# Joining the two half sums of a mixture-of-experts layer in PSUM, by identity products on TensorE, in place of an add on VectorE

## The chip, the cores and the metric

The kernel runs on one core of one Trainium2 chip. The metric is the device time in microseconds (us) of one execution, median of several runs. Its engines are TensorE (PE; its weight loads are PEld), VectorE (DVE), ScalarE (ACT), GpSimd (POOL) and SyncE (SP), which only issues DMAs here.

## The reference

Two post-norm transformer layers over 4 x 512 tokens of width 256, in float32. What matters here is the first feed-forward, a mixture of eight experts whose outputs are weighted by gates (two of the eight are not zero) and summed before one output projection:

```python
expert_out = gelu(einsum('bsh,ehd->ebsd', x, expert_w) + expert_b)
combined   = einsum('bse,ebsd->bsd', gates, expert_out)
y          = einsum('bsd,df->bsf', combined, out_w) + out_b
x          = layernorm(x + y)
```

## The kernel before

The 2048 tokens are 16 tiles of 128. The kernel is written out by hand for each engine, with semaphores; within an engine everything runs in the order in which it is written. All projections are three bf16 products (high x high, high x low, low x high, lines 468 to 470), which is why every activation is split into a bf16 high part (by ACT) and a low part (by DVE).

The first feed-forward is a software pipeline of steps, n = 0 to 17, from about 243 to 388 us of the span. Step n holds the experts of tile n, the first projection and norm of tile n + 6, and the end of tile n - 1 and n - 2. In PE's order a full step is:

1. the turn (transpose) "x1" of tile n + 5;
2. `experts(n, 0)` with the experts' bias (line 714), the first projection of tile n + 6, `experts(n, 1)`; every fourth step (n = 3, 7, 11) also router logits of four tiles, the "routed" steps below;
3. the turn "cc" of tile n + 7, then `experts(n, 2)`;
4. the turn **"cm"** of tile n - 1: the sum over the experts is turned so that it can be multiplied by `out_w`;
5. `experts(n, 3)`, the turn "x2" of tile n - 2, and `second_project(n - 1)`, which waits for DVE's low part of the turned sum.

First projections end with step 9, "cc" turns with step 8, "x1" turns with step 10. In step 16, where the experts are done, the first projections of layer 1 (`l1_project`: "k", "q", then "v" of one group) stand around the last "cm" turn, and step 17 has more of them.

The sum over the experts is made by two engines. DVE scales and adds the shares of experts 0 to 4 into `comb[t % 2]` (lines 1611 and 1614, semaphore `mul`), POOL those of experts 5 to 7 into `pc[t % 2]` (lines 2021 and 2026, semaphore `psum`). In step n DVE then joins the halves of tile n - 1, between `mix(n, 0)` and the residual add and statistics of `joined(n + 6, 1)`:

```python
dve.wait_ge(m["psum"], (NX - DVE_X - 1) * (t + 1))
dve.wait_ge(m["mul"], DVE_X * (t + 1))
dve.tensor_tensor(comb[t % 2], comb[t % 2], pc[t % 2], ALU.add).then_inc(m["join"], 1)
```

PE waits for `join` and turns the 256 columns in two fp32 transposes (line 667). ACT takes the high part from the bank (line 1062), DVE the low part (line 1381, `turned_low`, after the norms of the step). POOL may overwrite `pc` of tile t once tile t - 2 is joined.

DVE's order in a full step is: low part of x1, residual and statistics of tile n - 2 (lines 1507, 1509, 1510), `mix(n, 0)`, **join (line 1620)**, residual and statistics of tile n + 6, low part of cc, `mix(n, 1)`, the norms of tiles n - 2 and n + 6 (line 1516), low part of cm, `mix(n, 2)`, the next attention context (line 1493), low part of x2. In a routed step the choice of the experts (lines 1362 to 1376, 1546 to 1550) follows the low part of cm. POOL makes the inverse deviations for both norms (lines 2035, 2037).

Of the kernel before, what the change touches and what calls it, by code (L numbers as in the profile page):

```python
# [7 lines left out]
ALU = mybir.AluOpType  # L8
# [3 lines left out]
P = 128  # L12
E = 256
KE = E // P
# [3 lines left out]
NT = NB * TT  # L18
# [5 lines left out]
NX = 8  # L24
# [46 lines left out]
DVE_X = 5  # L71
# [18 lines left out]
TURNS = [(what, t) for at in sorted(EARLY_AT) for what, t in EARLY_AT[at] if what in ("cc", "x1")]  # L90
# [60 lines left out]
def build(nc, x_tok_d, x_t_d, wqkv_d, wall_d, const_d, bp_d, outb_d, b2_d, rb_d, eb_d, rw0_d, rw1_d, b1_d, out_d):  # L151
    ctx = ExitStack()
    with ctx:
# [3 lines left out]
        def sem(name):  # L157
            return ctx.enter_context(nc.semaphore(name))
# [46 lines left out]
        ident_f = consts[:, 0:P]  # L205
# [13 lines left out]
        lg = lg_sb[:, :].rearrange("p (t x) -> p t x", x=NX)  # L219
        rt = s_sb[0][:, 0:8 * NT * NX].rearrange("p (i c) -> p i c", i=8)  # L220
        gates = s_sb[0][:, 1152:1280].rearrange("p (t x) -> p t x", x=NX)
# [30 lines left out]
        def tiles(base, n, width, dt=F32):  # L252
            return [scr[:, base + width * i:base + width * (i + 1)].bitcast(dt) if dt != F32
                    else scr[:, base + width * i:base + width * (i + 1)] for i in range(n)]
# [5 lines left out]
        comb = tiles(1536, 2, E)  # L260
        tb_hi, tb_lo = tiles(12288, TB, P, BF16), tiles(13184, TB, P, BF16)
        ge = tiles(8192, 4, 512)
        pc = tiles(10240, 2, E)
# [27 lines left out]
        bank = [ctx.enter_context(nc.psum_tensor(f"bank{i}", [P, 512], F32)) for i in range(8)]  # L291
# [24 lines left out]
        def hold(eng, semaphore, value):  # L316

            if value > 0:
                eng.wait_ge(semaphore, value)
# [11 lines left out]
        l1_turned = [sem(f"l1_turned{i}") for i in range(2)]  # L331
        m = {n: sem(f"mix_{n}") for n in (
            "rc", "cc", "tp", "thi", "tlo", "o1", "o2", "r1", "r2", "agg1", "agg2", "rstd1", "rstd2", "x1", "x2", "xb",
            "lg", "lgc", "lgd", "ex", "gates", "f", "ge", "mul", "join", "pmul", "psum", "dve", "pool")}
        e = {n: sem(f"ffn_{n}") for n in (
            "tp", "thi", "tlo", "lg", "lgc", "lgd", "ex", "picks", "rank", "gates", "h", "ge", "hhi", "hlo",
            "y", "yr", "bg", "xb", "seq", "agg", "rstd", "x", "dve", "iota", "iotad", "rhi", "rlo", "pick",
# [4 lines left out]
        def turn_bank(i):  # L342
            return 7 if i < LONE_TURNS else i % 2
# [121 lines left out]
        def _(pe):  # L465
# [186 lines left out]
            def turn_mix(kind, t):  # L652

                i = TURNS.index((kind, t))
                if kind == "cc":
                    pe.wait_ge(m["cc"], t + 1)
                    src = cc[t % 2]
                elif kind == "cm":
                    pe.wait_ge(m["join"], t + 1)
                    src = comb[t % 2]  # L660
                else:
                    pe.wait_ge(m[kind], t + 1)
                    src = x_tok[:, t * E:(t + 1) * E]

                hold(pe, m["tlo"], i if i < LONE_TURNS else i - 1)
                for k in range(KE):
                    last = pe.transpose(bank[turn_bank(i)][:, k * P:(k + 1) * P], src[:, k * P:(k + 1) * P], ident_f)
                last.then_inc(m["tp"], 1)

            def project(out, t_hi, t_lo, base, n=E):  # L670
# [49 lines left out]
            for _ in range(WARM):  # L720
                pe.matmul(bank[7][:, :], ones_b[:, :], ones_b[:, :].unsqueeze(1).to_broadcast([P, TT, P]),
                          start=True, stop=True)
# [34 lines left out]
            for n in STEPS[len(EARLY):]:  # L757
                here, ahead, behind = 0 <= n < NT, n + LEAD + 1, n - 1
# [620 lines left out]
        def _(dve):  # L1379
# [4 lines left out]
            for i in range(2):  # L1384
                dve.memset(q_tok[i][:, :, M_ROW:ROWS], 0.0)
                last = dve.memset(k_tok[i][:, :, M_ROW + 3:ROWS], 0.0)
# [87 lines left out]
            def turned_low(kind, t):  # L1474
                i = TURNS.index((kind, t))
                dve.wait_ge(m["thi"], i + 1)
                if kind == "x2":
                    hi, lo = xt_hi[:, :, t * P:(t + 1) * P], xt_lo[:, :, t * P:(t + 1) * P]
                else:
                    his, los = {"cc": (ta_hi, ta_lo), "cm": (tc_hi, tc_lo), "x1": (tb_hi, tb_lo)}[kind]  # L1480
                    slot = t % (TB if kind == "x1" else 2)
                    hi, lo = kt(his[slot]), kt(los[slot])
                low(lo, kt(bank[turn_bank(i)][:, 0:E]), hi).then_inc(m["tlo"], 1)
# [35 lines left out]
            def sums_inverse(half):  # L1519

                heads = slice(half * NH // 2, (half + 1) * NH // 2)
                dve.wait_ge(a["vc"], (half + 1) * NT // 2)
                dve.reciprocal(rcc[:, heads, :], ctx0[:, heads, :, D0:VC].rearrange("p h q d -> p h (q d)")
                               ).then_inc(m["rc"], 1)
                dve.wait_ge(m["rc"], half + 1)
# [88 lines left out]
                        ins = dve.scalar_tensor_tensor(comb[t % 2], part, gate, comb[t % 2], ALU.mult, ALU.add)  # L1614
                    ins.then_inc(m["mul"], 1)

            def join_halves(t):
                dve.wait_ge(m["psum"], (NX - DVE_X - 1) * (t + 1))
                dve.wait_ge(m["mul"], DVE_X * (t + 1))
                dve.tensor_tensor(comb[t % 2], comb[t % 2], pc[t % 2], ALU.add).then_inc(m["join"], 1)  # L1620

            def l1_low(which, g, j=0):
                half = (g % 2) * TOK
                if which == "q":
                    hold(dve, c["phi"], 4 * g + j + 1)
                    low(qt_lo[j % 2], bank[4][:, :], qt_hi[j % 2]).then_inc(c["plo"], 1)
                elif which == "k":
                    hold(dve, c["kvh"], 2 * g + 1)
                    low(k1_lo[:, ds(half, TOK)], bank[5][:, :], k1_hi[:, ds(half, TOK)]
                        ).then_inc(c["kvl"], 1)  # L1630
                else:
                    hold(dve, c["kvh"], 2 * g + 2)
                    low(v1_lo[:, ds(half, TOK)], bank[5][:, :], v1_hi[:, ds(half, TOK)]
                        ).then_inc(c["kvl"], 1)

            for n in STEPS[len(EARLY):]:
                here, ahead, behind = 0 <= n < NT, n + LEAD + 1, n - 1
                if 0 <= n + LEAD < NT:
                    turned_low("x1", n + LEAD)
                if n == EARLY[-1] + 1:  # L1640
                    sums_inverse(1)
                if n == NT:
                    l1_low("k", 0)
                if 0 <= n - 2:
                    joined(n - 2, 2)
                routed = 0 <= n + 4 < NT and (n + 4) % TT == TT - 1
                if routed:
                    route((n + 4) // TT)
                if here:
                    mix(n, 0)  # L1650
                if 0 <= behind < NT:
                    join_halves(behind)
                if 0 <= ahead < NT:
                    joined(ahead, 1)
                if 0 <= n + LEAD + 2 < NT:
                    turned_low("cc", n + LEAD + 2)
                if n == NT:
                    l1_low("q", 0, 0)
                if here:
                    mix(n, 1)  # L1660
                if n == NT + 1:
                    l1_low("k", 1)
                if 0 <= n - 2:
                    norm(n - 2, 2)
                if n == NT + 1:
                    l1_low("v", 1)
                if 0 <= ahead < NT:
                    norm(ahead, 1)
                if 0 <= behind < NT:
                    turned_low("cm", behind)  # L1670
                if routed:
                    choose_first((n + 4) // TT)
                if n == NT:
                    l1_low("v", 0)
                if here:
                    mix(n, 2)
                if routed:
                    choose_second((n + 4) // TT)
                    gate((n + 4) // TT)
                if 0 <= n + LEAD + 3 < NT:  # L1680
                    context(n + LEAD + 3)
                if 0 <= n - 2:
                    turned_low("x2", n - 2)
# [179 lines left out]
            for i in range(2):  # L1863
                dve.wait_ge(e["yhi"], i + 1)
                cols = slice(2 * i * E, 2 * (i + 1) * E)
# [33 lines left out]
        def _(pool):  # L1899
            pool.memset(ones_b[:, :], 1.0).then_inc(c_ready, 1)  # L1900
            for i in range(2):
                last = pool.memset(k_tok[i][:, :, M_ROW:M_ROW + 3], -1.0)
# [108 lines left out]
            def mix(t, p):  # L2011

                pool.wait_ge(m["ge"], 4 * t + p + 1)
                if p == 2:

                    hold(pool, m["join"], t - 1)
                    if t % TT == 0:
                        pool.wait_ge(m["gates"], t // TT + 1)
                for x in range(max(2 * p, DVE_X), 2 * p + 2):
                    share = pc[t % 2] if x == DVE_X else pc_x[x % 2]  # L2020
                    pool.tensor_scalar(share, ge[p][:, (x % 2) * E:(x % 2 + 1) * E], gates[:, t, x:x + 1], 1.0,
                                       ALU.mult, ALU.mult).then_inc(m["pmul"], 1)
                    if x > DVE_X:
                        pool.wait_ge(m["pmul"], (NX - DVE_X) * t + x - DVE_X + 1)
                        hold(pool, m["psum"], (NX - DVE_X - 1) * t + x - DVE_X - 1)
                        pool.tensor_tensor(pc[t % 2], pc[t % 2], share, ALU.add).then_inc(m["psum"], 1)
# [146 lines left out]
```

## Time and profile before

| | |
|---|---|
| median of 3 runs | 892.85 us (892.05 to 892.85) |
| the profiled execution | 893.67 us, span 891.8 us |
| PE busy | 817.7 us, 92% of the span |
| DVE busy | 693.9 us, 78% |
| ACT, POOL busy | 496.5 us, 56%; 391.0 us, 44% |
| line 1620, the join, in the span | 16 instructions, 6.68 us |

Busy time of PE is a modelled sum: a matmul's end lies behind the start of the next one, so the distance between starts is the time that one takes when others follow. "Idle before" in square brackets is time of the engine ahead of an instruction, with what ended it.

### The profile page before, as it was taken

What the parts mean: (1) busy time and instruction counts of PE and PEld (TensorE: products, weight loads), DVE (VectorE), ACT (ScalarE), POOL (GpSimd) and SP (SyncE); (2) the same over time, 40 slices, a digit from 0 to 9 for tenths busy, and PEclk for the clock granted to TensorE, in tenths of its full rate; (3) what the DMA queues carried; (4) which work ended last, traced back from release to release, by engine and by line L of the source; (5) the groups of instructions that cost most, each with busy time, mean ns of one, the idle gap of its engine ahead of it and who ended that gap; (6) DMA issues with size and microseconds to landing.
All of it is one profiled execution on the core that took longest, in us unless ns stands there. A gap on an engine that the chain in (4) does not pass through costs nothing.

```text
span 891.8 us, 21987 instructions
## 1 busy us (share of the span) xinstructions
PE 817.7 (92%) x8131; PEld 514.1 (58%) x8227; DVE 693.9 (78%) x1921; ACT 496.5 (56%) x1181; POOL 391.0 (44%) x731
## 2 busy tenths in 40 slices
PE   7899999997898988979999999999999999997894
PEld 2455555553454544445566767666767766685374
DVE  4777777777688887678999888888888888856535
ACT  3577677765544534456666555656555565532243
POOL 4555667552365664523333343333333333333454
PEclk9999999999999999999999999999999999998998
DMA  5353333420000000016766565565556655550502
GB/s 167 107 127 91 94 84 97 121 31 8 2 1 1 1 1 1 1 28 122 119 123 123 97 104 104 99 101 98 96 99 103 104 105 97 97 91 1 95 1 95
DMA packets 219034, 67.70 MB, mean 76 GB/s; under 512 B 211360, under 2 KB 214704, under 8 KB 218928
## 3 DMA queue, kind: packets, MB, share of 16 engines
q1 hardware_dynamic: 218928, 66.29, 37.4%
q8 instruction: 66, 1.08, 0.5%
q14 instruction: 40, 0.33, 0.1%
HBM read 17.92 MB, written 4.19 MB: 25 GB/s over the span
## 4 chain that ended last, share of the span: by engine, by line
PE 71%; DVE 13%; issue 5%; DMA 3%; ACT 3%; POOL 3%; SPq 0%; POOLq 0%; DVEq 0%; ACTq 0%
PE bank L469 15%; PE bank L470 14%; PE bank L468 13%; PE bank L601 4%; PE bank L836 4%; PE bank L838 4%; PE bank L837 4%; DVE nm L1439 3%; DMA att<-w_lo 2%; PE bank L548 2%; PE bank L543 2%; PE bank L524 2%; PE bank L585 1%; DVE w_lo L1463 1%; DVE scr L1614 1%
## 5 line engine op out<-in xcount | busy, mean ns | idle before, releaser
L1157 ACT ACTIVATE att<-att,nm 128x512 f32<-128x512 f32 (+3 forms) x256 | 141.5, 553 | 104.4 <-DVE nm L1452 103.0
L1062 ACT ACTIVATE scr<-bank 128x512 bf16<-128x512 f32 (+3 forms) x210 | 111.5, 550 | 86.5 <-PE bank L838 44.2
L469 PE MATMUL bank<-w_lo,scr 128*128 128x256 bf16 (+1 forms) x478 | 144.0, 301 | 0.5
L468 PE MATMUL bank<-w_hi,scr 128*128 128x256 bf16 (+1 forms) x471 | 141.5, 300 | 2.9 <-DVE scr L1381 1.9
L470 PE MATMUL bank<-w_hi,scr 128*128 128x256 bf16 (+1 forms) x476 | 143.2, 301 | 0.1
L1439 DVE TENSOR_REDUCE nm<-bank 128x1 f32<-128x512 f32 (+3 forms) x256 | 110.6, 484 | 37.9 <-PE bank L548 37.8
L2070 POOL TENSOR_SCALAR wqkv_hi<-att,rr 128x512 bf16<-128x512 f32 (+3 forms) x128 | 66.1, 536 | 136.2 <-DVE rr L1469 136.2
L1452 DVE CUSTOM_DVE_ANT_0 att<-bank,consts 128x512 f32<-128x512 f32 (+3 forms) x256 | 113.2, 483 | 14.9 <-PE bank L470 14.9
L1108 ACT ACTIVATE att<-bank 128x512 f32<-128x512 f32 (+1 forms) x192 | 90.8, 528 | 50.1 <-PE bank L585 49.7
L1381 DVE TENSOR_TENSOR scr<-bank,scr 128x256 bf16<-128x256 f32 (+1 forms) x146 | 77.4, 540 | 51.0 <-ACT scr L1062 50.6
L2070 POOL TENSOR_SCALAR w_hi<-att,rr 128x512 bf16<-128x512 f32 (+3 forms) x128 | 66.1, 535 | 106.2 <-DVE rr L1469 106.2
L836 PE MATMUL bank<-att,w_hi 128*128 128x384 bf16 (+2 forms) x320 | 84.0, 273 | 4.5 <-DMA att<-w_lo 3.4
L837 PE MATMUL bank<-att,w_hi 128*128 128x384 bf16 (+2 forms) x320 | 87.2, 273 | 0.0
L838 PE MATMUL bank<-att,w_lo 128*128 128x384 bf16 (+2 forms) x320 | 83.9, 273 | 0.0
L469 PE MATMUL bank<-w_lo,w_hi 128*128 128x512 bf16 (+3 forms) x256 | 76.6, 299 | 0.5 <-DVE w_lo L1381 0.5
L470 PE MATMUL bank<-w_hi,w_lo 128*128 128x512 bf16 (+3 forms) x256 | 73.3, 299 | 0.0
L468 PE MATMUL bank<-w_hi 128*128 128x512 bf16 (+1 forms) x255 | 72.9, 299 | 0.2 <-DVE xt_lo L1381 0.2
L1381 DVE TENSOR_TENSOR w_lo<-bank,w_hi 128x512 bf16<-128x512 f32 x96 | 66.4, 691 | 8.2 <-ACT w_hi L1062 7.6
L1062 ACT ACTIVATE w_hi<-bank 128x512 bf16<-128x512 f32 x96 | 55.9, 582 | 28.1 <-PE bank L470 28.1
L469 PE MATMUL bank<-xt_lo,w_hi 128*128 128x512 bf16 x176 | 66.7, 379 | 3.1 <-DVE w_lo L1381 0.8
L1189 ACT ACTIVATE scr<-bank 128x512 f32<-128x512 f32 x64 | 38.1, 597 | 55.9 <-PE bank L470 35.0
L470 PE MATMUL bank<-xt_hi,w_lo 128*128 128x512 bf16 x176 | 66.7, 379 | 0.0
(242 smaller groups left out, 2014.7 us busy)
## 6 DMA issues: line engine op xcount, KB each, us to landing
scr<-wall_in SPq DMA_DIRECT2D x19, 512.0 KB, 4.7
v_by_token<-scr SPq DMA_DIRECT2D x16, 128.0 KB, 1.8
scr<-v_by_token SPq DMA_DIRECT2D x16, 128.0 KB, 3.5
x_tok<-x_tok_in SPq DMA_DIRECT2D x4, 512.0 KB, 5.1
scr<-x_t_in SPq DMA_DIRECT2D x3, 512.0 KB, 5.7
out<-x_tok SPq DMA_DIRECT2D x3, 512.0 KB, 2.6
scr<-wqkv_in SPq DMA_DIRECT2D x2, 384.0 KB, 3.6
att<-w_hi SPq DMA_TRANSPOSE x32, 3.4
```

Of the source, the lines that this page charges most:

```text
L468: pe.matmul(out, l_hi, r_hi, start=start, stop=False, skip_group_check=check)
L469: pe.matmul(out, l_hi, r_lo, start=False, stop=False, skip_group_check=check)
L470: return pe.matmul(out, l_lo, r_hi, start=False, stop=stop, skip_group_check=check)
L836: pe.matmul(out, v1_hi[:, vs], hi, start=(kt, q0) == (0, 0), stop=False, skip_group_check=True)
L837: pe.matmul(out, v1_hi[:, vs], lo, start=False, stop=False, skip_group_check=True)
L838: last = pe.matmul(out, v1_lo[:, vs], hi, start=False, stop=(kt == TT - 1), skip_group_check=True)
L1062: return act.activation(out, in_, ACT.Copy)
L1157: last = act.activation(at, at, ACT.Exp, bias=nm[:, j % 2, qt:qt + 1], scale=-1.0, accum_out=rs[:, j % 2, qt:qt + 1])
L1381: return dve.tensor_tensor(out, bank_cols, hi, ALU.subtract)
L1439: last = dve.tensor_reduce(nm0[:, p % 2, h, qt:qt + 1], bank[n % 2][:, col:col + w], AX.X, ALU.max)
L1452: last = dve.tensor_tensor_reduce(s_sb[j % 2][:, S_OFF[qt]:S_OFF[qt] + w], bank[turn][:, col:col + w], mask[:, 512 - w:512], -scale, HUGE, ...
L2070: pool.tensor_scalar(ps_hi[j % 2][:, at], s_sb[j % 2][:, at], rr[:, j % 2, qt:qt + 1], 1.0, ALU.mult, ALU.mult).then_inc(c["row"], 1)
```

## The change

The join leaves DVE. PE no longer transposes the joined sum: it multiplies each half by the fp32 identity, both into the same columns of the bank, so that PSUM adds them. There are four fp32 matmuls (two halves, two column blocks) in place of two transposes. The first pair waits for DVE's last share (`mul`), the second for POOL's last add (`psum`). POOL's guard on `pc` becomes the turn "cm" of tile t - 2.

```diff
                 elif kind == "cm":
-                    pe.wait_ge(m["join"], t + 1)
+                    pe.wait_ge(m["mul"], DVE_X * (t + 1))
                     src = comb[t % 2]
...
                 hold(pe, m["tlo"], i if i < LONE_TURNS else i - 1)
-                for k in range(KE):
-                    last = pe.transpose(bank[turn_bank(i)][:, k * P:(k + 1) * P], src[:, k * P:(k + 1) * P], ident_f)
+                if kind == "cm":
+                    halves = (comb[t % 2], pc[t % 2])
+                    for part, half in enumerate(halves):
+                        if part == 1:
+                            pe.wait_ge(m["psum"], (NX - DVE_X - 1) * (t + 1))
+                        for k in range(KE):
+                            cols = slice(k * P, (k + 1) * P)
+                            last = pe.matmul(bank[turn_bank(i)][:, cols], half[:, cols], ident_f,
+                                             start=(part == 0 and k == 0), stop=(part == 1 and k == KE - 1),
+                                             skip_group_check=True)
+                else:
+                    for k in range(KE):
+                        last = pe.transpose(bank[turn_bank(i)][:, k * P:(k + 1) * P], src[:, k * P:(k + 1) * P], ident_f)
                 last.then_inc(m["tp"], 1)
...
-            def join_halves(t):
-                dve.wait_ge(m["psum"], (NX - DVE_X - 1) * (t + 1))
-                dve.wait_ge(m["mul"], DVE_X * (t + 1))
-                dve.tensor_tensor(comb[t % 2], comb[t % 2], pc[t % 2], ALU.add).then_inc(m["join"], 1)
...
-                if 0 <= behind < NT:
-                    join_halves(behind)
...
                 if p == 2:
-                    hold(pool, m["join"], t - 1)
+                    if t >= 2:
+                        pool.wait_ge(m["tp"], TURNS.index(("cm", t - 2)) + 1)
```

On TensorE, at the turn "cm" of the tile before, between two pieces of experts (512 columns each) and ahead of the turn "x2"; before:

```order
L470 MATMUL bank<-w_hi,scr 128x512
L667 MATMUL bank<-consts,scr 128x128 [waits mix_tlo,mix_join]
L667 MATMUL bank<-consts,scr 128x128
L468 MATMUL bank<-w_hi,scr 128x512
L469 MATMUL bank<-w_lo,scr 128x512
```

and now:

```order
L470 MATMUL bank<-w_hi,scr 128x512
L673 MATMUL bank<-consts,scr 128x128 [waits mix_tlo,mix_mul]
L673 MATMUL bank<-consts,scr 128x128
L673 MATMUL bank<-consts,scr 128x128 [waits mix_psum]
L673 MATMUL bank<-consts,scr 128x128
L468 MATMUL bank<-w_hi,scr 128x512
```

Two instructions have become four, with the second wait in the middle; what stands around them is as before.

## Rows read from the trace of the kernel before

**Rows 1.** Page, part 1: busy time, share of the span, instructions.

```profile
PE 817.7 (92%) x8131; PEld 514.1 (58%) x8227; DVE 693.9 (78%) x1921; ACT 496.5 (56%) x1181; POOL 391.0 (44%) x731
```

**Rows 2.** Steps 6 to 12 and 15: stretch: length, busy us (instructions), granted clock, DMA.

```profile
core 0: us, PE busy (x) PEld busy (x) DVE busy (x) ACT busy (x) POOL busy (x), PEclk, DMA share, GB/s
294.22:302.34 8.12, 7.92 (x48) 4.46 (x49) 7.06 (x20) 3.60 (x9) 5.48 (x11) 1.00 0.00 0
302.34:312.45 10.11, 8.71 (x71) 4.93 (x73) 8.21 (x23) 6.89 (x13) 6.68 (x13) 1.00 0.01 2
312.45:322.93 10.48, 8.55 (x48) 4.22 (x49) 9.82 (x34) 3.73 (x9) 4.60 (x9) 1.00 0.00 2
322.93:330.64 7.71, 7.66 (x45) 4.20 (x46) 6.27 (x18) 2.71 (x7) 5.32 (x11) 1.00 0.01 2
330.64:337.58 6.94, 6.89 (x41) 3.69 (x41) 5.65 (x14) 3.20 (x8) 4.68 (x9) 1.00 0.00 0
337.58:345.95 8.37, 7.53 (x64) 3.92 (x62) 5.42 (x16) 6.19 (x10) 4.56 (x9) 1.00 0.01 2
345.95:354.82 8.87, 6.88 (x39) 3.38 (x39) 8.28 (x27) 2.58 (x6) 3.59 (x7) 1.00 0.00 0
...
368.23:374.94 6.71, 6.66 (x40) 3.46 (x39) 4.65 (x13) 2.94 (x7) 3.87 (x7) 1.00 0.01 2
```

**Rows 3.** Timeline, step 6: POOL, PE, DVE: start us, us, engine line op [idle before].

```profile
296.65 0.72 POOL L2026 TENSOR_TENSOR scr<-scr 128x256 f32<-128x256 f32 x1
...
300.29 0.38 PE L667 MATMUL bank<-consts,scr 128*128 128x128 f32 x2
300.51 0.38 PE L468 MATMUL bank<-w_hi,scr 128*128 128x512 bf16 x1
...
301.80 0.38 PE L667 MATMUL bank<-consts,x_tok 128*128 128x128 f32 x2
302.34 0.28 PE L468 MATMUL bank<-w_hi,scr 128*128 128x256 bf16 x1 [0.15 <-DVE scr L1381]
...
301.87 0.41 DVE L1381 TENSOR_TENSOR scr<-bank,scr 128x256 bf16<-128x256 f32 x1
```

**Rows 4.** The only other fp32 matmuls, line 601: groups (busy us, mean ns), and timeline.

```profile
L601 PE MATMUL bank<-att,scr 128*17 128x512 f32 x128 | 16.9, 598 | 0.0
...
L601 PE MATMUL bank<-att,scr 128*17 128x128 f32 x128 | 6.4, 273 | 0.0
...
154.40 0.62 PE L601 MATMUL bank<-att,scr 128*17 128x512 f32 x4
...
154.84 0.61 PE L601 MATMUL bank<-att,scr 128*17 128x512 f32 x4
```

**Rows 5.** Timeline of PE and DVE, step 4, around the turn cm.

```profile
282.81 0.44 PE L667 MATMUL bank<-consts,scr 128*128 128x128 f32 x2 [0.68 <-DVE scr L1620]
...
282.33 0.42 DVE L1620 TENSOR_TENSOR scr<-scr 128x256 f32<-128x256 f32 x1
282.67 0.42 DVE L1507 TENSOR_TENSOR x_tok<-bank,x_tok 128x256 f32<-128x256 f32 x1
```

**Rows 6.** Timeline of PE and DVE, step 12, around the turn cm.

```profile
353.03 0.44 PE L667 MATMUL bank<-consts,scr 128*128 128x128 f32 x2 [1.94 <-DVE scr L1620]
...
354.23 0.41 DVE L1381 TENSOR_TENSOR scr<-bank,scr 128x256 bf16<-128x256 f32 x1
```

**Rows 7.** Timeline of step 16: POOL's last add, PE's turn, POOL, DVE, PE.

```profile
377.43 0.72 POOL L2026 TENSOR_TENSOR scr<-scr 128x256 f32<-128x256 f32 x1
...
379.79 0.44 PE L667 MATMUL bank<-consts,scr 128*128 128x128 f32 x2 [1.45 <-DVE scr L1620]
...
379.87 0.55 POOL L2037 TENSOR_TENSOR rstd<-var_e,neg_half 128x1 f32<-128x1 f32 x1
...
382.24 0.69 DVE L1381 TENSOR_TENSOR w_lo<-bank,w_hi 128x512 bf16<-128x512 f32 x1 [1.03 <-ACT w_hi L1062]
...
383.21 0.38 PE L469 MATMUL bank<-xt_lo,w_hi 128*128 128x512 bf16 x1 [0.76 <-DVE w_lo L1381]
```

More of the change, by code:

```diff
@@ L333, in build @@
             "rc", "cc", "tp", "thi", "tlo", "o1", "o2", "r1", "r2", "agg1", "agg2", "rstd1", "rstd2", "x1", "x2", "xb",
-            "lg", "lgc", "lgd", "ex", "gates", "f", "ge", "mul", "join", "pmul", "psum", "dve", "pool")}
+            "lg", "lgc", "lgd", "ex", "gates", "f", "ge", "mul", "pmul", "psum", "dve", "pool")}
         e = {n: sem(f"ffn_{n}") for n in (
```

## The prediction

> **What bounds the kernel now.** I read the page's busy shares first: PE is busy 92% of the span, DVE 78% [rows 1]. That only says that work put on PE is dangerous; what the change is worth is decided in the first feed-forward, where it acts. So I cut that stage at the starts of `second_project`, one stretch per step [rows 2], and looked in the timeline for what PE waits for in each. There are three kinds of steps.
>
> *Plain steps* (1, 2, 5, 6; step 6 is the first stretch of rows 2): 8.12 us. The turn cm at 300.29 takes 0.22 us, until the next matmul at 300.51, and waits for nothing: the join is early. PE's only wait comes after the turn x2 (301.80 + 0.22 = 302.02), until 302.34, when DVE's low part of cm (line 1381) is there [rows 3]: 0.32 us. So PE's own work is 8.12 - 0.32 = 7.80 us. DVE reaches that low part late because in the same step it waited for ACT's high part of cc; the join lies before that wait, so taking it away only lengthens the wait. Step 9 has no cc turn, 7.80 - 0.22 = 7.58 of its 7.71 us: 0.13 us of slack. Step 10 has no first projection (six matmuls of 256 columns, about 0.65 us): 6.93 of 6.94, none. Steps 13 to 15 have no x1 turn either: 6.71 of 6.71, none [rows 2]. These nine steps are PE's.
>
> *Routed steps* (3, 7, 11; second and sixth stretch of rows 2): ACT and DVE wait on each other for the router. PE is busy 8.71 of 10.11 us, and 7.53 of 8.37; the modelled ends flatter PE, so 1.4 and 0.8 us are floors of its idle time, and it lies behind the turn cm, ahead of the turn x2.
>
> *Steps after them* (4, 8, 12; third and seventh stretch): DVE has the gates to make and is busy 9.82 of 10.48 us in step 8 [rows 2]. Only here PE waits for the join. A modelled end lies 0.16 us behind the moment at which the next matmul could start (0.38 against 0.22), so in step 4 PE is free at 282.81 - 0.68 - 0.16 = 281.97 [rows 5], and in step 12 at 353.03 - 1.94 - 0.16 = 350.93 [rows 6]. The last turn, in step 16, also waits for it, 1.45 us [rows 7].
>
> **The price of the new turn.** Two transposes take 0.22 us, 0.11 each [rows 3]. An fp32 matmul that is not a transpose stands in the trace at line 601 alone. The program has 64 of them with 512 columns, and the trace 128 records: each matmul is recorded twice. The first four records start at 154.40 and their four partners at 154.84, and over the group 512 columns take 598 ns and 128 columns 273 ns, that is 0.85 ns a column for each record, two cycles at 2.4 GHz (granted clock 1.00) [rows 2, 4]. So 128 columns cost 2 x 0.108 = 0.216 us, twice a transpose, and four of them 0.86 us: **+0.64 us a turn**, 16 times 10.3 us of PE's time. I take this value because columns, type and engine are the same; what differs is the weights: 17 columns at line 601, 128 here. That loads of 128 fp32 weights keep up with 128 columns is shown only for transposes (0.11 each, load included [rows 3]). Bounds: if a matmul against the identity were one record like a transpose, +0.22 us; if its weight loads could not hide (8 x 0.11 on top), +1.50 us. A gain there is excluded, since two instructions become four.
>
> The Trainium skill, in "TensorE: Matmul & The Clock Gate", Terms, has the transpose mode as four times faster for fp32. By that a turn would take 4 x 4 x 0.11 = 1.7 us and not 0.86, the second rival below.
>
> **What leaves DVE.** One add of 0.34 us (282.33 to 282.67 [rows 5]) in each of 16 steps. In plain steps and steps 9, 10, 13 to 15 it hides behind waits for ACT and is worth nothing. In steps 4 and 8 everything behind it on DVE, down to the norm for x2 and the low part of cm that PE waits for, moves 0.34 us ahead. The extra waits are free: POOL's last add of a tile is ready well before the turn (296.65 + 0.72 against 300.29 in step 6 [rows 3]) in every step but 16, and POOL's new guard is a turn of the step before.
>
> **The sum**, step by step, from one `second_project` to the next:
>
> - Steps 1, 2, 5, 6: +0.64 less the 0.32 of slack, +0.32 each: +1.28. The low part of cm is not made late: the turn now ends at 300.29 + 0.86 + 0.17 of pipeline, ACT needs 0.4, done at 301.7, DVE comes at 301.87 [rows 3].
> - Step 9: +0.51. Step 10: +0.64. Steps 13 to 15: +1.92.
> - Steps 3, 7, 11: 0, PE's idle time takes the 0.64.
> - Steps 4 and 8: -0.34 each, -0.68. PE turns at 281.97, is through the experts at 284.1 and waits for the norm as before.
> - Step 12: the turn starts at 350.93 and ends 351.79; 1.30 for `experts(12, 3)`; the next wait is the low part of cm, 354.23 less 0.34 = 353.89 [rows 6], which reaches PE 0.47 later (as in step 6: 301.87 to 302.34), 354.36 in place of 354.82: -0.46.
> - Step 16: PE is free at 379.79 - 1.45 - 0.16 = 378.18, POOL's last add ends at 377.43 + 0.73 [rows 7], so the turn starts at 378.22, ends at 379.08, and "v" of layer 1 follows 0.98 us earlier than now (it stood behind 379.79 + 0.27). Its low part, now at 382.24, releases PE at 383.21. It could come 0.97 earlier; POOL's deviation (379.87 + 0.55 [rows 7]), which does not move, lets the norm and the low part of cm (some 0.33 us each) be over by 381.11, just in time for 381.27. -0.97.
>
> Together +1.28 + 0.51 + 0.64 + 1.92 - 0.68 - 0.46 - 0.97 = **+2.24 us**. Some 4.35 us more on the path, 2.1 us back. The profiled execution took 893.67 us (span 891.8 and 1.9 around it), 0.8 above the median of 892.85; the sum is a difference, so I put it on the median: 895.1 us.
>
> The Trainium skill's "Perfetto Trace Analysis", Transposes, tells to use a transpose for a transpose and not a matmul. That speaks against this change; it sets no price, and changes no term above.
>
> **Rivals.**
>
> 1. *The turn is nearly free, not slower.* Each identity product is one record of 0.11 us: +0.22 a turn. For it: a transpose of the same shape is one record. Against it: all fp32 matmuls of line 601 have two [rows 4]. Plain steps hide it in 0.32; step 9 +0.09, step 10 +0.22, steps 13 to 15 +0.65; the gains are -0.68, -0.46 and in step 16 -1.13 (until POOL's deviation binds). Sum -1.3: 891.5 us. It decides as soon as a turn costs less than about 0.3 us more than now. Chance 0.08.
> 2. *The turn takes 1.7 us.* Either full weight loads don't hide, or the products stream four times slower than transposes; both give +1.50. Steps 1, 2, 5, 6 +1.18 each, step 9 +1.37, step 10 +1.50, steps 13 to 15 +4.5, step 11 +0.55, steps 4, 8, 12 still -1.14, step 16 -0.11: +11.4, 904.2 us. For it: no row shows two passes with 128 fp32 weight columns. Against it: transposes with the same load sustain 0.11. Chance 0.10.
> 3. *A new wait.* The price is right, but the later end of the turn makes ACT's high part meet a gelu in its order, and DVE's low part of cm slips in plain steps, where I have 0.17 us of margin; some 0.3 us in nine steps, +5: 897.8 us. Chance 0.10.
> 4. *The forecast*, +0.8 to +3.9 us: chance 0.72. Terms that can slide by half a microsecond each are step 16, step 12, and the length of DVE's instructions beside POOL.
>
> **How the numbers follow.** A measurement here tells a change from none from about 0.2%, 1.8 us. The forecast's +2.24 lies just beyond: of its 0.72 I give 0.48 to slower and 0.24 to within. Rivals 2 and 3 add 0.20 to slower, rival 1 gives 0.05 to within and 0.03 to faster. Faster 0.03, same 0.29, slower 0.68. The range reaches from 893.2 (the low end of the forecast, less a little) to 898.2 (rival 3 in), leaving out rivals 1 and 2.
>
> **What the profile after would show.** Per turn eight fp32 records and eight weight loads, 0.86 us from the first to the next bf16 matmul; if 0.43 or 1.7, rival 1 or 2. Steps 1, 2, 5, 6 at 8.44 us, PE without a wait; steps 13 to 15 at 7.35; steps 4 and 8 shorter by 0.3 with PE waiting only for the norm; step 12 near 8.3; "v" of layer 1 one microsecond nearer to the last experts. The stage as a whole 2 us longer and everything behind it shifted, not changed. I am wrong if PE still waits for line 1381 in plain steps, or if a stretch behind 390 us changes its length.

## The result, and the profile after

The changed kernel takes 895.16 us (median of 10 runs, 892.59 to 900.49) against 892.28 us for the kernel before (10 runs, 889.27 to 892.9, made beside it). The ratio is 1.0039, 95% interval 1.002 to 1.0058: slower by 2.9 us. The profiled execution took 895.28 us with a span of 893.5 us, against 893.67 and 891.8 before. The repeat at the end of the experiments gave 1.0035 (1.0017 to 1.0053).

Two spans that differ by 1.7 us do not show where 2.6 us went, because the parts outside the first feed-forward vary from program to program: the stage began at 243.26 us before and begins at 241.72 now (between 239.25 and 243.15 in the kernels below), on work that the change doesn't touch. So each kernel is compared here by its **stage**: from the first "x1" turn of step 0 to the first matmul of 128 columns of "v" in step 17. It was 142.61 us (243.26 to 385.87) and is 145.24 us (241.72 to 386.96): +2.63 us. In the repeat it was 145.27; in the two pairs of repeated kernels this measure agrees to 0.05 us or better.

Part 1 of the page of the kernel after, busy time by engine (answers to [rows 1]):

```profile
PE 825.8 (92%) x8226; PEld 525.6 (59%) x8323; DVE 688.5 (77%) x1905; ACT 498.2 (56%) x1181; POOL 389.3 (44%) x731
```

DVE lost 16 instructions and 5.4 us, PE gained 95 records. The program puts 96 more there (128 for the products, less 32 for the transposes); one is missing from the trace.

The same steps as in [rows 2], from one `second_project` to the next, kernel after (steps 6 to 12 and 15, columns as there):

```profile
293.49:301.96 8.47, 8.42 (x55) 5.23 (x54) 6.80 (x19) 3.70 (x9) 5.20 (x10) 1.00 0.01 2
301.96:311.91 9.95, 9.38 (x80) 5.66 (x78) 7.45 (x22) 7.16 (x13) 5.51 (x11) 1.00 0.00 0
311.91:322.33 10.42, 9.00 (x54) 5.01 (x55) 9.77 (x33) 4.00 (x9) 5.35 (x10) 1.00 0.01 2
322.33:330.59 8.26, 8.21 (x51) 5.00 (x53) 6.47 (x17) 2.70 (x7) 5.66 (x11) 1.00 0.00 1
330.59:338.19 7.60, 7.55 (x48) 4.39 (x47) 4.85 (x13) 3.44 (x8) 4.29 (x8) 1.00 0.01 2
338.19:346.56 8.37, 8.18 (x70) 4.63 (x68) 4.47 (x14) 6.02 (x10) 3.84 (x7) 1.00 0.00 0
346.56:354.88 8.32, 7.61 (x44) 4.04 (x45) 7.63 (x26) 3.30 (x7) 4.38 (x8) 1.00 0.01 2
...
369.65:377.03 7.38, 7.33 (x46) 4.17 (x45) 4.32 (x11) 3.05 (x7) 3.87 (x7) 1.00 0.01 2
```

Against [rows 2]: step 6 went from 8.12 to 8.47 us, step 9 from 7.71 to 8.26, step 10 from 6.94 to 7.60 and step 15 from 6.71 to 7.38, always with the granted clock at 1.00. The routed step 7 got shorter (10.11 to 9.95), step 8 after it hardly (10.48 to 10.42), step 12 by half a microsecond (8.87 to 8.32).

Timeline of PE, step 6 of the kernel after, and DVE's and POOL's lines that answer to [rows 3]:

```profile
299.56 1.05 PE L673 MATMUL bank<-consts,scr 128*128 128x128 f32 x8
300.45 0.38 PE L468 MATMUL bank<-w_hi,scr 128*128 128x512 bf16 x1
...
301.74 0.38 PE L678 MATMUL bank<-consts,x_tok 128*128 128x128 f32 x2
301.96 0.27 PE L468 MATMUL bank<-w_hi,scr 128*128 128x256 bf16 x1
```

```profile
301.14 0.41 DVE L1392 TENSOR_TENSOR scr<-bank,scr 128x256 bf16<-128x256 f32 x1
...
296.00 0.73 POOL L2031 TENSOR_TENSOR scr<-scr 128x256 f32<-128x256 f32 x1
```

The turn cm is eight records and takes 0.89 us (299.56 to 300.45), where it took 0.22. `second_project` follows the turn x2 at 301.96 = 301.74 + 0.22, without a wait: the 0.32 us that [rows 3] show there are gone. DVE's low part of cm starts at 301.14 and is over in time. PE now has no gap in this step; the step is its work.

The line of the products on PE and on PE's weight loads (duration in ns, least, median and most), kernel after:

```profile
L673 PEld LDWEIGHTS bank<-consts,scr x128: 190/192/192, 253.8 to 380.9; 128*128 128x128 f32 x128
L673 PE MATMUL bank<-consts,scr x128: 272/275/275, 254.0 to 381.1; 128*128 128x128 f32 x128
```

128 matmuls and 128 weight loads for 64 instructions: each is recorded twice, as at line 601 [rows 4].

The turn cm in steps 4 (PE) and 12 (PE and DVE), which answer to [rows 5] and [rows 6], kernel after:

```profile
281.18 1.05 PE L673 MATMUL bank<-consts,scr 128*128 128x128 f32 x8
282.07 0.38 PE L468 MATMUL bank<-w_hi,scr 128*128 128x512 bf16 x1
```

```profile
351.54 1.05 PE L673 MATMUL bank<-consts,scr 128*128 128x128 f32 x8
...
354.55 0.44 PE L678 MATMUL bank<-consts,x_tok 128*128 128x128 f32 x2 [0.66 <-DVE x_tok L1527]
...
354.42 0.41 DVE L1392 TENSOR_TENSOR scr<-bank,scr 128x256 bf16<-128x256 f32 x1
```

Neither turn waits any more, where they waited 0.68 and 1.94 us. In step 12 the wait moved to the turn x2, for DVE's norm (0.66 us).

Step 16, POOL's last add, the turn, and DVE's part of "v" (answers to [rows 7]):

```profile
379.52 0.73 POOL L2031 TENSOR_TENSOR scr<-scr 128x256 f32<-128x256 f32 x1
...
380.27 1.05 PE L673 MATMUL bank<-consts,scr 128*128 128x128 f32 x8
...
383.33 0.69 DVE L1392 TENSOR_TENSOR w_lo<-bank,w_hi 128x512 bf16<-128x512 f32 x1
```

The turn comes with no wait, 0.21 us after the matmul before it. The low part of "v" starts 6.30 us after `second_project` of step 15 (377.03 to 383.33), where it was 7.30 us (374.94 [rows 2] to 382.24 [rows 7]): one microsecond back, with a turn that is 0.62 us longer in it (0.89 us, for 0.27 from 379.79 to 380.06 before).

### The profile page after: what moved, and what is told of

Read it like the earlier page. It is cut to its first block, busy times and chain, and to the rows that moved or that the text cites. A ratio compares the mean times of both kernels' runs of the same rounds, so it can differ in the third digit from the quotient of the medians.

```text
span 893.5 us, 22146 instructions
## 1 busy us (share of the span) xinstructions
PE 825.8 (92%) x8226; PEld 525.6 (59%) x8323; DVE 688.5 (77%) x1905; ACT 498.2 (56%) x1181; POOL 389.3 (44%) x731
## 4 chain that ended last, share of the span: by engine, by line
PE 72%; DVE 13%; issue 5%; POOL 3%; DMA 3%; ACT 3%; SPq 0%; POOLq 0%; DVEq 0%; ACTq 0%
PE bank L469 15%; PE bank L470 14%; PE bank L468 13%; PE bank L601 4%; PE bank L847 4%; PE bank L849 4%; PE bank L848 4%; DVE nm L1450 3%; DMA att<-w_lo 3%; PE bank L548 2%; PE bank L543 2%; PE bank L524 2%; PE bank L585 1%; DVE w_lo L1474 1%; DVE scr L1625 1%
```

## The experiments

Four questions: what the turn costs by itself, what DVE's relief is worth by itself, why steps 3 and 4 gave back less than DVE lost, and whether a mixture of the two forms beats both kernels. For each kernel the stage is given, since the medians of whole runs carry the variation outside it.

**Only the relief.** The two transposes of `comb` alone, with the waits of the change; POOL's half is left out of the sum:

```diff
-                    halves = (comb[t % 2], pc[t % 2])
-                    for part, half in enumerate(halves):
...
+                    pe.wait_ge(m["psum"], (NX - DVE_X - 1) * (t + 1))
+                    for k in range(KE):
+                        last = pe.transpose(bank[turn_bank(i)][:, k * P:(k + 1) * P], src[:, k * P:(k + 1) * P], ident_f)
```

> As the changed kernel, but the turn cm is two transposes of DVE's half alone (POOL's half is left out of the sum; the turn still waits for it). It shows what taking the join from DVE brings when PE pays nothing. Stage = first x1 turn of step 0 to the first v matmul of step 17: 142.61 us before, 145.24 with the change. Theory 1 (step by step: DVE's add counts only where PE waits for DVE): plain steps as before (8.12), steps 3 with 4 and 7 with 8 together -0.2 each, step 12 -0.5, step 16 -1.1: stage 140.6, time -2.0 us against before. Theory 2 (the add was on the path in every step): 16 x 0.34 = -5.4 us.

Measured: 888.82 us, ratio 0.9972 (0.9956 to 0.9988), stage 140.36 us. The relief alone is worth 2.25 us: steps 3 and 4 together 20.25 us for 20.58 before, steps 7 and 8 likewise 20.25 for 20.59, steps 15 to 17 1.16 us less, step 12 only 0.07 less, and steps 1 and 9 0.22 and 0.14 less. So the sum was near what I expected (140.6), but not its terms: the pairs gave 0.33 us each and not 0.2, step 12 almost nothing for 0.5, and steps 1 and 9, for which I had nothing, use PE's slack. In the changed kernel PE's own longer turn takes that slack, so the gain of steps 1 and 9 is not there.

**Half the price.** Two fp32 products of `comb` in place of the two transposes; POOL's half is left out here too:

```diff
-                    for part, half in enumerate(halves):
...
+                    pe.wait_ge(m["psum"], (NX - DVE_X - 1) * (t + 1))
+                    for k in range(KE):
+                        cols = slice(k * P, (k + 1) * P)
+                        last = pe.matmul(bank[turn_bank(i)][:, cols], comb[t % 2][:, cols], ident_f,
+                                         start=(k == 0), stop=(k == KE - 1), skip_group_check=True)
```

> As the changed kernel, but the turn cm is two identity products of DVE's half (POOL's half left out): four fp32 records, 0.44 us a turn in place of 0.89. Theory 1: plain steps hide all of it in their 0.32 us of slack (8.12 us again); step 9 +0.1, step 10 +0.2, steps 13 to 15 +0.2 each, gains as in gain_only: stage 141.6, time -1.0 us against before. Theory 2 (time follows PE's work): half of the change's cost, 16 x 0.22 = +3.5 less 5.4.

Measured: 891.61 us, 1.0005 (0.999 to 1.0021), stage 141.69 us. The turn in step 6 of this kernel (timeline of PE):

```profile
298.99 0.61 PE L670 MATMUL bank<-consts,scr 128*128 128x128 f32 x4
299.43 0.38 PE L468 MATMUL bank<-w_hi,scr 128*128 128x512 bf16 x1
```

0.44 us for two products, 0.22 each: the price goes by the number of products, and a step with 0.32 us of slack takes one such step up unseen (plain steps 8.12 us again), while those without pay it (6.93 to 6.94 for 6.70 in steps 13 and 14). The pairs are the surprise: 20.54 and 20.53 us, so with half the price next to nothing of the 0.33 us is left there, less than the 0.18 and 0.22 that the full price leaves. A cost that simply grows with the turn can't do that; the next but one experiment takes it up.

**Only the price.** The join stays on DVE and PE does the four products on top, so POOL's half is added twice; POOL's guard is the changed kernel's:

```diff
+                if kind == "cm":
+                    for part, half in enumerate((comb[t % 2], pc[t % 2])):
+                        for k in range(KE):
+                            cols = slice(k * P, (k + 1) * P)
+                            last = pe.matmul(bank[turn_bank(i)][:, cols], half[:, cols], ident_f,
...
-                    hold(pool, m["join"], t - 1)
+                    if t >= 2:
+                        pool.wait_ge(m["tp"], TURNS.index(("cm", t - 2)) + 1)
```

> The kernel before with the join kept on DVE; after it PE makes the four identity products (POOL's half is added twice, so the sum is another). It shows the price without the relief. Theory 1: steps 1, 2, 5, 6 +0.35 each, 9 +0.54, 10 +0.67, 13 to 15 +0.67 each, 12 and 16 +0.67 each because the turn still starts late, 3, 4, 7, 8, 11 nothing: +5.9 us, stage 148.5. Theory 2 (every turn pays): 16 x 0.67 = +10.7 us.

Measured: 899.88 us, 1.008 (1.005 to 1.0109), stage 148.52 us, +5.91. The plain steps, 9, 10, 13 and 14 are those of the changed kernel to 0.01 us. Price and relief apart make +5.91 - 2.25 = +3.66 us, together +2.63: the difference is 1.0 us. The last stretch (from the experts' bias of step 15 to the end of the stage) and step 12 are +1.39 and +0.38 with the price alone, -1.16 and -0.07 with the relief alone, and -0.33 and -0.54 with both: 1.4 us less than the two apart. Steps 1 and 9 give back 0.36 of it, because there the relief alone was worth something. That the stage came out at the 148.5 I expected is in part luck: step 12 paid 0.38 and not 0.67, and the pairs paid 0.14 and 0.12 where I had nothing.

**What steps 3 and 4 are short of.** The trace of DVE's choice of the experts differs in the lengths of single instructions. Timeline of DVE in step 3, and of POOL beside it, kernel before:

```profile
275.17 0.41 DVE L1381 TENSOR_TENSOR scr<-bank,scr 128x256 bf16<-128x256 f32 x1
275.50 0.46 DVE L1362 SCALAR_TENSOR_TENSOR att<-att,consts 128x32 f32<-128x32 f32 x1
...
276.67 0.83 DVE L1614 SCALAR_TENSOR_TENSOR scr<-scr,att 128x256 f32<-128x256 f32 x1
...
279.52 0.42 DVE L1493 TENSOR_TENSOR scr<-scr 128x256 f32<-128x256 f32 x1
...
274.60 0.49 POOL L2021 TENSOR_SCALAR scr<-scr,att 128x256 f32<-128x256 f32 x1
...
276.45 0.77 POOL L2026 TENSOR_TENSOR scr<-scr 128x256 f32<-128x256 f32 x1
```

And kernel after, the same stretch, with POOL's:

```profile
274.10 0.41 DVE L1392 TENSOR_TENSOR scr<-bank,scr 128x256 bf16<-128x256 f32 x1
...
275.09 0.64 DVE L1377 SCALAR_TENSOR_TENSOR att<-att 128x32 f32<-128x32 f32 x1
275.76 0.64 DVE L1625 SCALAR_TENSOR_TENSOR scr<-scr,att 128x256 f32<-128x256 f32 x1
...
276.54 0.50 DVE L1384 TENSOR_TENSOR att<-att,r1c 128x32 f32<-128x32 f32 x1
...
278.74 0.42 DVE L1504 TENSOR_TENSOR scr<-scr 128x256 f32<-128x256 f32 x1
```

```profile
274.37 0.50 POOL L2026 TENSOR_SCALAR scr<-scr,att 128x256 f32<-128x256 f32 x1 [0.67 <-ACT scr L1200]
...
276.22 0.77 POOL L2031 TENSOR_TENSOR scr<-scr 128x256 f32<-128x256 f32 x1
```

From the low part of cm to the add for the attention context DVE needs 4.35 us before (275.17 to 279.52) and 4.64 after (274.10 to 278.74): 0.29 us more in a stretch whose instructions are the same (the norms just before it give 0.16 back, so DVE leaves the stretch 0.12 to 0.13 us later than before). My theory: DVE's instructions with two inputs from SBUF are drawn out while POOL works (an instruction of the kind of L1377 takes 0.18 to 0.19 us elsewhere in the stretch), and the longer turn delays the last gelu of the step, so that POOL waits (0.67 us) and its shares reach further into the choice. To test it, POOL's shares in the tiles of the routed steps are cut to 8 of 256 columns, in both kernels (the other columns of POOL's half of these tiles are left out, so this measures and saves nothing that could be kept):

```diff
+QUIET = (3, 7, 11)
...
-                    share = pc[t % 2] if x == DVE_X else pc_x[x % 2]
+                    w = 8 if t in QUIET else E
+                    share = (pc[t % 2] if x == DVE_X else pc_x[x % 2])[:, 0:w]
```

> The kernel before, with POOL's shares and adds for tiles 3, 7 and 11 cut to 8 of 256 columns (the rest of POOL's half of these tiles is left out). In steps 3 and 4 some DVE instructions are longer than their kind: line 1362 0.46 for 0.18, line 1614 0.83 for 0.48 us; in step 12 line 1364 0.56, 1366 0.41, 1614 1.02. Theory A (DVE instructions with two SBUF inputs are held while POOL works on SBUF): they fall to their kind; steps 3 with 4 and 7 with 8 (bias matmul to bias matmul) go from 20.59 to about 20.0, steps 11 with 12 from 17.25 to about 16.1, other steps as before. Theory B (PE or ACT hold them): no change.

> The changed kernel with the same cut. Its long DVE instructions in steps 3 and 4 sum to 0.3 us more than before (0.64, 0.64, 0.50). Theory A: the 0.34 us of the join comes through whole once POOL is quiet: steps 3 with 4 about 20.0 - 0.34 = 19.7 against 20.40 with POOL at work, and in step 12 the advantage over before_quiet is only what the join's place gives, 0.3 to 0.5. Theory B (the longer turn in step 3 itself delays step 4): the pair stays about 0.2 below before_quiet, not 0.34.

Measured: 887.09 and 891.89 us, one run each; stages 139.63 and 142.39 us. Timeline of DVE, step 3, kernel before with a quiet POOL:

```profile
271.55 0.41 DVE L1384 TENSOR_TENSOR scr<-bank,scr 128x256 bf16<-128x256 f32 x1
271.87 0.18 DVE L1365 SCALAR_TENSOR_TENSOR att<-att,consts 128x32 f32<-128x32 f32 x1
...
272.76 0.48 DVE L1617 SCALAR_TENSOR_TENSOR scr<-scr,att 128x256 f32<-128x256 f32 x1
...
275.26 0.42 DVE L1496 TENSOR_TENSOR scr<-scr 128x256 f32<-128x256 f32 x1
```

The same instructions take 0.18 and 0.48 us in place of 0.46 and 0.83, and the stretch 3.71 us in place of 4.35. That the shorter instructions are the whole effect, and not POOL's own chain ending sooner, can be added up: from the experts' bias of step 3 to that of step 5 DVE's instructions sum to 0.87 us less and the pair is 0.86 us shorter (20.58 to 19.72); in steps 11 and 12 they sum to 1.25 us less and the time is 1.25 us shorter (17.25 to 16.00). The other theory, that PE or ACT hold DVE, had foreseen no change. So the stretching by POOL is shown: 2.98 us of stage over three tiles (142.61 to 139.63).

With POOL quiet, steps 3 and 4 are 19.72 us before and 19.44 after: the change saves 0.28 us there, where with POOL at work it saves 0.18 (steps 7 and 8: 0.31, for 0.22). The expectation for the changed kernel had the whole 0.34. Of what is missing with POOL at work, 0.12 us are carried out of step 3 by DVE's lengths, and some 0.03 are lost in step 4 ahead of the join's old place. With POOL quiet 0.04 us are missing at that place and 0.06 at the end of the pair; what that small rest is stays open.

The other two kernels agree. With the price alone DVE leaves step 3 0.13 us later, with the same lengths as in the changed kernel (0.64, 0.64, 0.50), and the pair is 0.14 longer: PE's longer turn costs nothing there by itself. With half the price the stretch takes 4.80 us (273.74 to 278.54) for 4.35, the pair keeps 0.04 of the relief, and that is its surprise explained. Step 12 gains 0.24 us with POOL quiet (7.70 to 7.46), less than the 0.3 to 0.5 expected.

**The products only where they pay.** PE waits for the join in the turns of tiles 3, 7, 11 and 15 alone (steps 4, 8, 12, 16). There the join leaves DVE; elsewhere it stays, with transposes:

```diff
+IN_PSUM = (3, 7, 11, 15,)
+JOINS = [t for t in range(NT) if t not in IN_PSUM]
...
-                if kind == "cm":
+                if kind == "cm" and t in IN_PSUM:
...
+                if 0 <= behind < NT and behind not in IN_PSUM:
+                    join_halves(behind)
```

> Identity products only for tiles 3, 7, 11, 15 (their turns are in steps 4, 8, 12, 16, where PE waited for the join); all other tiles joined on DVE and transposed as before. Theory 1: all the gains without the cost: steps 3+4 and 7+8 -0.2 each, 12 -0.5, 16 -1.0: stage 140.7, time -1.9 us against before, faster than both kernels. Theory 2 (each turn costs 0.67 less 0.34): +1.3 us.

Measured: 889.67 us, 0.9972 (0.9951 to 0.9993), stage 140.71 us. Timeline of DVE, step 3 (the turn there is a transpose, as before):

```profile
274.46 0.40 DVE L1399 TENSOR_TENSOR scr<-bank,scr 128x256 bf16<-128x256 f32 x1
274.79 0.46 DVE L1380 SCALAR_TENSOR_TENSOR att<-att,consts 128x32 f32<-128x32 f32 x1
...
275.95 0.83 DVE L1632 SCALAR_TENSOR_TENSOR scr<-scr,att 128x256 f32<-128x256 f32 x1
...
278.82 0.42 DVE L1511 TENSOR_TENSOR scr<-scr 128x256 f32<-128x256 f32 x1
```

4.36 us, the durations of the kernel before to 0.01 us, and steps 3 and 4 take 20.25 us for 20.58: the whole 0.33 to 0.34 comes through when the turn of step 3 is short. Its step 12 is 0.21 us shorter than before, against 0.54 in the changed kernel. The stage is the one expected (140.7), again with terms that make up for each other: 0.33 a pair and not 0.2, 0.21 in step 12 and not 0.5.

**Step 12.** The extra there, I supposed, came from the long turn of step 11, which moves POOL's adds along. So the products also in the turn of tile 10:

```diff
-IN_PSUM = (3, 7, 11, 15,)
+IN_PSUM = (3, 7, 10, 11, 15,)
```

> Identity products for tiles 3, 7, 10, 11 and 15. Tile 10 turns in step 11, where PE waits 0.95 us for the norm anyway, so its 0.67 costs nothing. Theory A (where POOL's work falls beside DVE's decides step 12: 8.87 before, 8.66 in hybrid4, 8.33 in the changed kernel, whose step 11 turn is long and makes POOL's adds later): step 12 falls from 8.66 to about 8.33, stage 140.4, time -2.2 us against before. Theory B (step 12's gain comes from the join alone): step 12 stays at 8.66, stage 140.7.

Measured: 890.05 us, 0.9987 (0.9964 to 1.0009), stage 140.40 us, step 12 8.32 us, 0.55 under before. DVE and POOL around the choice in this kernel's step 12, and DVE's in the kernel before:

```profile
341.82 0.40 DVE L1399 TENSOR_TENSOR scr<-bank,scr 128x256 bf16<-128x256 f32 x1
...
342.58 0.20 DVE L1382 TENSOR_TENSOR att<-consts,r1c 128x32 f32<-128x32 f32 x1
342.82 0.27 DVE L1384 SCALAR_TENSOR_TENSOR att<-att 128x32 f32<-128x32 f32 x1
...
346.41 0.41 DVE L1399 TENSOR_TENSOR xt_lo<-bank,xt_hi 128x256 bf16<-128x256 f32 x1
...
342.56 0.49 POOL L2040 TENSOR_SCALAR scr<-scr,att 128x256 f32<-128x256 f32 x1 [0.81 <-ACT scr L1207]
```

```profile
345.49 0.41 DVE L1381 TENSOR_TENSOR scr<-bank,scr 128x256 bf16<-128x256 f32 x1
...
346.33 0.56 DVE L1364 TENSOR_TENSOR att<-consts,r1c 128x32 f32<-128x32 f32 x1
346.92 0.41 DVE L1366 SCALAR_TENSOR_TENSOR att<-att 128x32 f32<-128x32 f32 x1
...
350.41 0.42 DVE L1381 TENSOR_TENSOR xt_lo<-bank,xt_hi 128x256 bf16<-128x256 f32 x1
```

The stretch takes 4.59 us (341.82 to 346.41) in place of 4.92: POOL waits 0.81 us for its gelu just while DVE does its two-input instructions. The same delay that hurts in step 3 helps in step 11. It is an accident of alignment, not relief. In whole time this kernel and the one with four turns can't be told apart.

**The add earlier on DVE.** If what pays is only that DVE's low parts and norms come sooner, moving the add may do as much. In steps 4, 8, 12 and 16 it goes ahead of the residual of tile n - 2:

```diff
+                sooner = n in (4, 8, 12, 16)
+                if sooner:
+                    join_halves(behind)
...
-                if 0 <= behind < NT:
+                if 0 <= behind < NT and not sooner:
```

> The kernel before; in steps 4, 8, 12 and 16 DVE joins the halves first, ahead of the residual of tile n - 2, so that PE no longer waits for the join but DVE does the same work. If PE's wait for the join was what cost time, steps 3+4, 7+8 and 12 fall as in hybrid4 (20.25, 8.66). Theory 1 says DVE's 0.34 of work is what binds in 4, 8 and 12 (no change there, 20.59 and 8.8), and only step 16, where PE waits 1.45 us, gains: from step 15's bias matmul to the first v matmul of step 17 14.8 for 15.60. Stage 141.7.

Measured: 890.37 us (one run), stage 142.02 us. Steps 3 and 4 keep 20.57 us (10.11 + 10.46), the last stretch falls from 15.60 to 14.77, and step 12 grows by 0.27 to 9.14, 0.34 over what I had said. In step 16 it is the wait for the add that counts, and an earlier add removes 0.83 of the 1.01 us that the products remove there, with no product at all; in steps 4 and 8 it is DVE's amount of work, and order doesn't help.

Step 12 shows two more things. The add stands there between two instructions of `mix`, and DVE needs 0.74 us from the start of the one to the start of the next with the add between them, and 0.58 to 0.59 without: taking it out is worth 0.16 us, putting it elsewhere costs 0.34. And once PE doesn't wait for the join, POOL's shares can come earlier and meet DVE's norm, as here and with the relief alone. Norm in step 12 before, then norm and POOL with the relief alone:

```profile
353.91 0.40 DVE L1516 TENSOR_SCALAR x_tok<-x_tok,mv,rstd 128x256 f32<-128x256 f32 x1
```

```profile
350.04 0.57 DVE L1521 TENSOR_SCALAR x_tok<-x_tok,mv,rstd 128x256 f32<-128x256 f32 x1
...
350.54 0.73 POOL L2025 TENSOR_TENSOR scr<-scr 128x256 f32<-128x256 f32 x1
```

**The three kernels in one comparison.**

> The changed kernel once more, on the same chip and beside the same runs of the kernel before as hybrid4_again, so that the three stand in one comparison. Theory (turn +0.67 us, most of the relief in steps 3+4 and 7+8 given back to the contention with GpSimd): +2.6 us of stage against before, 145.2 us, hence some 0.3% slower; the whole time 2.5 to 3 us above before. Rival (the +0.39% of the first comparison was partly a difference of chips or rounds, the change costs only my 2.24 us of step sum or less): within 0.2%.

> The products only in the turns of tiles 3, 7, 11 and 15, the add on VectorE for the others, once more beside after_again. Theory: stage 140.7 us, 1.9 us under before and 4.5 under after; 0.2% faster than before, 0.5% faster than after. Rival (the gain seen in two comparisons came from the stretches outside the stage, which vary by 2 us between programs without relation to the edit): ratio to before on either side of 1.000, though the stage is again 140.7.

Measured beside the same 23 runs of the kernel before (891.72 us): changed kernel 895.42 us, 1.0035 (1.0017 to 1.0053), stage 145.27; products in four turns 890.64 us, 0.9987 (0.9965 to 1.0009), stage 140.76. The two intervals don't meet: the mixture is faster than the change. That it is faster than the kernel before is shown in the stage (-1.9 us twice) and by the first comparison; the second interval reaches over 1, so as whole time it stands at one to two microseconds, at the edge of what can be measured.

## Why the prediction was right, and where it was off

The time (895.16 us for 895.1), the sign and the place were right, and the sum of the steps was +2.24 us for a measured +2.63 of stage. The closeness of the time is in part luck: 895.1 stood on a median of 892.85 us from three runs; on the 892.28 of the ten runs the same sum gives 894.5. The difference was +2.9 us for a forecast +2.24, and the ten runs of a kernel spread over 3.6 us (before) and 7.9 us (after).

| steps | predicted | measured |
|---|---|---|
| 1, 2, 5, 6 | +1.28 | +1.35 |
| 9; 10; 13 to 15 | +0.51; +0.64; +1.92 | +0.54; +0.67; +2.02 |
| 3 with 4, 7 with 8 | -0.68 | -0.40 |
| 11 | 0 | 0 |
| 12 | -0.46 | -0.54 |
| 16 | -0.97 | -1.00 |

- *"+0.64 us a turn"*: right in its mechanism, two records for each product, each at two cycles a column (0.111 us for 128 columns, 0.87 ns a column; a bf16 record of 512 columns takes 0.215 us, 0.42 ns a column). It measured 0.89 us for 0.86 and 0.67 for the difference, in step 6 and in the steps without slack. A record took 0.111 us and not 0.108, as a transpose does. The Trainium skill ("FP8 and Floating Point Precision", TensorE Precision Notes) has true fp32 as four passes through the array. An estimate from it, at a column a cycle and 2.4 GHz, is 4 x 128 columns = 0.213 us for a product, and the trace has 0.22.
- *The transpose as four times faster* (the Trainium skill, "TensorE: Matmul & The Clock Gate", Terms), the second rival: refuted here. A product takes 0.22 us and a transpose of the same tile 0.11, a factor of 2, so the turn took 0.89 us and not 1.7.
- *The first rival* (one record, nearly free) fell with the 128 records of 64 instructions. Its point of decision, about 0.3 us a turn, agrees with the kernel of half the price: +0.22 us a turn, whole time 1.0005.
- *The third rival*, a late low part of cm in plain steps: no such wait (301.14 + 0.41 against 301.96). PE is without a gap.
- *Steps 3, 7, 11 at 0 and steps 4 and 8 at -0.34 each*: this term was mis-sized. The pair must be read together, and it gave -0.18 and -0.22. The prediction let everything behind the join "move 0.34 us ahead" with its length unchanged. The choice of the experts was drawn out by 0.29 us beside POOL, and DVE's norms in step 3 got 0.16 shorter (1.30 to 1.14 us), because POOL's work came later. With the transposed turn in step 3 the whole 0.34 came through. PE still waited 0.30 us for the low part of cm in step 4, as before, and not for the norm alone.
- *Step 12*: the path was the one I gave. `second_project` follows the start of the low part of cm by 0.46 us (354.42 to 354.88) for the 0.47 that I took, and the slack of 0.12 was right. But the low part came 0.42 us earlier and not 0.34, and for another reason: 0.34 from the alignment in step 11, and only 0.08 from the add, where the sum had 0.34 from the add and nothing from step 11. That the two nearly agree is luck. "Length of DVE's instructions beside POOL" stood among the terms that could slide, without a number.
- *Step 16*: right. PE is free, and POOL's last add ended (379.52 + 0.73), when the turn starts at 380.27, and the rest was "just in time" as forecast: DVE waited 0.38 us for POOL's deviation, and the low part of cm ended at 382.79 + 0.42 = 383.21, ahead of the low part of "v" at 383.33.
- *"Everything behind it shifted, not changed"*: 506.0 us from the stage's end to the end of the span before, 506.5 after, within the 505.5 to 507.7 of the other kernels.

## What to carry to other kernels

An add moved from DVE into PSUM by identity products costs 0.67 us of PE for a turned fp32 tile of 128 x 256, against 0.34 us of DVE; so count the steps in which PE waits for that add, and move it in those alone. The Trainium skill's rule to use a transpose for a transpose ("Perfetto Trace Analysis", Transposes) held here in 11 turns of 16. It did not in the four where the add was late, nor at tile 10, where the products gained 0.33 us by the accident of step 11. At the last of the late ones an earlier place for the add brings most of the gain without any product: try that first. Before an engine is relieved, see whether its chain is long by work or by contention: smaller shares for POOL in three of sixteen tiles took 3.0 us from the stage (by leaving work out), the relief in all sixteen 2.25 us.

## What the runs showed of the hardware

- A 128 x 32 instruction of DVE with two SBUF inputs takes 0.18 to 0.19 us, and up to 0.64 us beside POOL's tensor instructions; one of 128 x 256 (line 1614) 0.48 us, and up to 1.02. With POOL quiet those of step 3 fall back to 0.18 and 0.48. The norm (line 1516: one tensor and two values per partition, all in SBUF) goes from 0.40 to as much as 0.81. Low parts and residuals of 128 x 256, which have one of their two inputs in PSUM, keep their 0.39 to 0.42 us, though 44 of them ran beside POOL in the stage before. The Trainium skill ("GPSIMD Engine Reference", Key points) names this contention for DVE instructions in a 2-port perf mode or with two SBUF inputs. For two inputs the trace agrees; in which mode the norm ran no run here shows. The size is what I had not expected.
- Loads of 128 fp32 weight columns take 190 to 192 ns ahead of a product and 140 to 141 ns (median) ahead of a transpose, and in both cases the records follow each other at 0.11 us.
- A delay of POOL by two thirds of a microsecond can cost DVE 0.3 us in the choice of the experts (step 3) or save it 0.3 us (step 11), by which instructions it lands on.
